# Score matmuls of two heads in alternating row tiles, and vector work moved to ScalarE and GpSimd

## What is computed

```python
h = relu(layernorm(x)); x = x + L0(h)   # deg*(h Wi + b) + A (h Wj)
h = relu(layernorm(x)); x = x + L1(h)   # one-head graph attention
h = relu(layernorm(x)); x = x + L2(h)   # 8-head dot-product attention, masked by adj
h = relu(layernorm(x)); x = x + L3(h)   # 4 attention heads + 1 output head, FFN, layernorm
```

## Time and profile before

| | us |
|---|---|
| median of 3 runs | 1984.97 (1984.79 to 1987.22) |
| the profiled execution | 1986.96 |
| its span, first to last instruction | 1985.3 |
| PE busy | 1872.7 (94% of the span) |
| DVE busy | 1727.5 (87%) |
| ACT busy | 1450.5 (73%) |
| POOL busy | 607.5 (31%) |

### The profile page before, as it was taken

How to read it: one execution, slowest core, us unless ns; L and a number is a source line. 1 busy time by engine, 2 the same in 40 slices (tenths; PEclk the granted TensorE clock), 3 DMA queues, 4 the chain that set the end, 5 groups by cost and what they waited for, 6 DMA issues and landing times.

```text
span 1985.3 us, 45990 instructions
## 1 busy us (share of the span) xinstructions
PE 1872.7 (94%) x15944; PEld 1772.0 (89%) x15944; DVE 1727.5 (87%) x6095; ACT 1450.5 (73%) x3378; POOL 607.5 (31%) x756
## 2 busy tenths in 40 slices
PE   0789999999999999999999999999999999999965
PEld 0789999999999999999999999999999999998864
DVE  6678999999999999999999999999999989999743
ACT  2347787777777877787787777778877777787653
POOL 4112332323333223333332323333223333322222
PEclk8789999999999999999999999999999999999887
DMA  5000000000000000000000000000000000000000
GB/s 158 9 13 11 23 23 17 18 23 13 22 23 23 18 17 23 23 12 22 23 21 19 18 23 12 22 23 23 17 18 23 23 12 23 18 17 18 12 16 11
DMA packets 31206, 43.85 MB, mean 22 GB/s; under 512 B 3328, under 2 KB 26880, under 8 KB 30976
## 3 DMA queue, kind: packets, MB, share of 16 engines
q1 hardware_dynamic: 30976, 40.91, 6.4%
HBM read 32.38 MB, written 8.52 MB: 21 GB/s over the span
## 4 chain that ended last, share of the span: by engine, by line
PE 78%; DVE 8%; ACT 5%; issue 5%; POOL 1%; DMA 0%; DVEq 0%; ACTq 0%; POOLq 0%; SPq 0%
PE ps L900 54%; PE ps L929 13%; PE ps L1094 8%; PE ps L1113 3%; DVE lg L1367 2%; ACT pT L861 2%; ACT ea L808 1%; DVE tb L1296 1%; DVE cx L1387 1%; ACT pb L853 1%; ACT ea L799 0%; PE ps L1002 0%; DVE fu L1333 0%; DVE hT L1220 0%; DVE pT L1375 0%
## 5 line engine op out<-in xcount | busy, mean ns | idle before, releaser
L853 ACT ACTIVATE pb<-lg,hmin 128x256 f32<-128x256 f32 x512 | 232.1, 503 | 67.4 <-DVE hmin L1367 67.0
L1094 PE MATMUL ps<-kp,qp 32*128 32x256 f32 x1536 | 251.7, 296 | 3.3 <-DVE hmin L1367 1.7
L708 POOL TENSOR_SCALAR ea<-ea,rs 128x256 f32<-128x256 f32 x256 | 144.2, 575 | 356.7 <-DVE rs L1317 356.6
L735 POOL TENSOR_TENSOR fu<-fu,b_b 128x256 f32<-128x256 f32 x64 | 45.9, 738 | 674.1 <-PE ps L929 674.1
L861 ACT ACTIVATE pT<-ps 128x512 f16<-128x512 f32 x256 | 151.1, 590 | 133.3 <-PE ps L1113 67.4
L1367 DVE CUSTOM_DVE_ANT_0 lg<-ps,maskp 128x256 f32<-128x256 f32 x512 | 195.3, 419 | 55.6 <-PE ps L1094 55.6
L1094 PEld LDWEIGHTS ps<-kp,qp 32*128 32x128 f32 x1536 | 199.3, 186 | 39.4 <-issue 12.3
L900 PE MATMUL ps<-wout,hid 128*128 128x256 f32 x1536 | 219.7, 289 | 3.3 <-ACT hid L867 2.6
L900 PE MATMUL ps<-pT,whs 128*128 128x256 f32 x1536 | 212.6, 288 | 4.8 <-DVE pT L1326 3.0
L900 PE MATMUL ps<-wh,hT 128*128 128x256 f32 x1536 | 205.0, 286 | 0.4 <-DVE cols L1267 0.3
L692 POOL TENSOR_TENSOR rstd<-ve,pow_half 128x2 f32<-128x2 f32 x160 | 118.4, 741 | 280.4 <-DVE ve L1198 280.3
(11 more groups left out here) (180 smaller groups left out, 4683.3 us busy)
## 6 DMA issues: line engine op xcount, KB each, us to landing
tbc<-t_dram SPq DMA_DIRECT2D x32, 512.0 KB, 3.6
xin<-x_in SPq DMA_DIRECT2D x32, 256.0 KB, 2.8
out<-xs SPq DMA_DIRECT2D x32, 256.0 KB, 2.2
t_dram<-tb SPq DMA_DIRECT2D x128, 1.0 KB
xs<-a_heads SPq DMA_DIRECT2D x4, 128.0 KB, 6.3
pT<-a_heads SPq DMA_DIRECT2D x4, 128.0 KB, 5.0
lg<-W_out SPq DMA_DIRECT2D x2, 256.0 KB, 5.5
tb<-adj SPq DMA_DIRECT2D x1, 256.0 KB, 2.8
```

Source lines behind the costliest of these rows:

```text
L708: last = pool.tensor_scalar(ea(g)[:, c, :], ea(g)[:, c, :], rs[g][:, c:c + 1], 1.0, ALU.mult, ALU.mult)
L853: last = act.activation(pb[h % 2][:, c, :], lg[h % 2][:, c, :], ACT.Exp, bias=hmin[h % 2][:, c:c + 1], scale=-1.0)
L1094: last = pe.matmul(bank(BA)[:, c, :], qp[r, a, oc, blk(c)], kp[r, b, oc, :], start=(n == 0), stop=(n == 2))
```

## The change

The scores of two heads become one step of 12 matmuls. Heads `2p` and `2p+1` alternate matmul by matmul; they lie in neighbouring 32-row tiles of the array, and the odd head writes bank `BB` instead of `BA`. Each head's transposed probabilities go to its own bank (`head_bank`). The pair's scores wait for `pT16_lo` of the pair before; `p_T` waits no longer for the other head. ScalarE writes the normalised rows of the four layers' norms from `rstd` and a new `nmr` (minus mean times `rstd`), which POOL computes with two instructions of one column behind `inv_std`. POOL also takes `normal`, and the low parts of layer 3's last head and of the FFN. `stats` gets a wait for the rows of the batch before at its head. The planner gets costs for all this and new `LEAD` values.

```diff
-            a("inv_std", n, PO, 0.78, ("var", n))
+            a("inv_std", n, PO, 1.1 if n < 4 else 0.78, ("var", n))
...
-            a("rows", 2, VE, 0.65, ("inv_std", 2), ago("rows_T", 3))
+            a("rows", 2, SC, 0.8, ("inv_std", 2), ago("rows_T", 3))
...
-                a("scores", h, TE, 0.7, ("q_lo", 0), ("k_lo", 0), ("smin", h - 1))
-                a("smin", h, VE, 0.69, ("scores", h), ("s_exp", h - 2))
+                if h % 2 == 0:
+                    a("scores", h // 2, TE, 0.8, ("q_lo", 0), ("k_lo", 0), ("pT16_lo", h - 1))
+                a("smin", h, VE, 0.69, ("scores", h // 2), ("s_exp", h - 2))
                 a("s_exp", h, SC, 0.8, ("smin", h), ("p_T", h - 2))
-                a("p_T", h, TE, 0.44, ("s_exp", h), ("pT16_lo", h - 1))
+                a("p_T", h, TE, 0.44, ("s_exp", h))
...
-                    a("normal", h // 2, VE, 0.27, ("gather", h // 2))
+                    a("normal", h // 2, PO, 0.5, ("gather", h // 2))
...
-                a("hid_lo", g, *((VE, 0.7) if g == HG else (PO, 1.25)), ("hid_hi", g))
+                a("hid_lo", g, PO, 1.25, ("hid_hi", g))
...
-            a("f1_lo", 0, VE, 0.7, ("f1_hi", 0))
+            a("f1_lo", 0, PO, 1.25, ("f1_hi", 0))
...
-        GRAIN, LEAD = 0.02, (42.0, 28.0, -2.0, 23.0)
+        GRAIN, LEAD = 0.02, (58.0, 49.0, 48.0, 52.0)
...
+        def head_bank(h):
+            return BB if h % 2 else BA
...
-                    pool.tensor_tensor(rstd[n][:], ve[n][:], pow_half[:], ALU.pow).then_inc(rstd_ready[n], 1)
+                    ins = pool.tensor_tensor(rstd[n][:], ve[n][:], pow_half[:], ALU.pow)
+                    if n < 4:
+                        ins.then_inc(rstd_made[n], 1)
+                        pool.wait_ge(rstd_made[n], u + 1)
+                        for c in range(C):
+                            ins = pool.tensor_scalar(nmr[n][:, c:c + 1], mv[n][:, c, 0:1], rstd[n][:, c:c + 1], -1.0,
+                                                     ALU.mult, ALU.mult)
+                    ins.then_inc(rstd_ready[n], 1)
...
+                def low_of_ffn(_, u):
+                    pool.wait_ge(f1_hi, u + 1)
+                    pool.tensor_tensor(f1p[:, 1], rb5[:], f(f1p[:, 0]), ALU.subtract).then_inc(f1_lo, 1)
+
+                def normalise(p, u):
+                    pool.wait_ge(o_used, of(u, p, HQ // 2))
...
+                        last = pool.tensor_tensor(two_heads(p)[:, hh], two_heads(p)[:, hh],
+                                                 r.broadcast_to([P, C, DH]), ALU.mult)
...
+                def norm_rows(n, u):
+                    t = row_of(n)
+                    act.wait_ge(rstd_ready[n], u + 1)
...
+                    for c in range(C):
+                        last = act.activation(rows_src(t)[:, c, :], norm_src(n, u)[:, c, :], ACT.Identity,
+                                              bias=nmr[n][:, c:c + 1], scale=rstd[n][:, c:c + 1])
+                    last.then_inc(rows_ready[t], 1)
...
-                def scores(h, u):
-                    if h == 0:
+                def scores(p, u):
+                    if p == 0:
                         pe.wait_ge(q_lo, u + 1)
                         pe.wait_ge(k_lo, u + 1)
                     else:
-                        pe.wait_ge(min_ready, of(u, h - 1, HQ))
-                    r, oc = slice(DH * (h % 4), DH * (h % 4) + DH), h // 4
+                        pe.wait_ge(pT16_lo, of(u, 2 * p - 1, HQ))
                     for c in range(C):
                         for n, (a, b) in enumerate(PARTS):
-                            last = pe.matmul(bank(BA)[:, c, :], qp[r, a, oc, blk(c)], kp[r, b, oc, :],
-                                             start=(n == 0), stop=(n == 2))
+                            for h in (2 * p, 2 * p + 1):
+                                r, oc = slice(DH * (h % 4), DH * (h % 4) + DH), h // 4
+                                last = pe.matmul(bank(head_bank(h))[:, c, :], qp[r, a, oc, blk(c)], kp[r, b, oc, :],
+                                                 start=(n == 0), stop=(n == 2))
                     last.then_inc(s_done, 1)
...
                     pe.wait_ge(p_done, of(u, h, HQ))
-                    if h:
-                        pe.wait_ge(pT16_lo, of(u, h - 1, HQ))
-                    transpose_to(BB, pb[h % 2]).then_inc(p_turned, 1)
+                    transpose_to(head_bank(h), pb[h % 2]).then_inc(p_turned, 1)
...
                 def stats_of(n, u):
+                    if n < 4 and u:
+                        dve.wait_ge(rows_ready[row_of(n)], u)
```

90 lines of the change are left out of this document (35 added, 55 removed).

## The result

The changed kernel takes 1937.49 us (median; 1935.54 to 1940.87) against 1985.03: ratio 0.9756, 95% interval 0.9739 to 0.9773. It is faster, by 2.4% and not by the forecast 5.3%. The profiled execution has a span of 1936.5 us.

What follows compares the result with a forecast made beforehand. PE was taken as the bound in mid-run. From a span of 1985.3 us: -46.2 (fewer score groups), -90.6 (overlap), +40 (taken back by others), -10 (end) gave 1878.5, forecast as 1880 us; range 1844 to 1955.

Steps and rivals of the forecast that it cites:

- The view and the bound: Mid-run: PE waits for nobody, 57.8 of 58.0 us a batch; DVE 53.1, ACT 45.3, POOL 18.9.
- Parts 1 and 2: Layer scores on PE: half as many groups, -46.2 us; alternating tiles run two heads side by side, -90.6 us.
- The rivals on the tiles: Score matmuls: loads in series (1934 us, 0.13), no overlap (1946, 0.09), tile changes costing like mode changes (2223, 0.07).
- Part 3: Work leaving DVE: 190.5 us, 6.0 a batch, from 53.1 to 47.1; gains nothing by itself but makes room.
- Part 4: Work arriving elsewhere: ACT 45.3 to 48.9 us a batch, POOL 18.9 to between 23 and 33, staying free.
- Part 5: Mid-run: PE at 53.5 us a batch, ACT 91%, DVE 88%, layer 3's chain 93%; 1.3 us x 31 lost, +40.
- The filling of the pipeline I leave as it is: Start of the run, while the pipeline fills: no separate term in the sum for a change there.
- The bound of 3 us a batch: Upper bound on what other engines and layer 3's chain take back in mid-run, almost the whole overlap; lower bound 0.
- The second rival: Mid-run: overlap works, but layer 3's chain or ACT holds the period at 56.5 us a batch; 1931 us, chance 0.11.
- the sign of its own forecast: Mid-run: PE busy at 97 to 98% and a batch every 54.8 us.
- The signs of being wrong: Mid-run: PE waiting for `pT16_lo` before the scores, or for ACT's normalised rows, would show the prediction wrong.
- Part 6: End of the run: PE's 14.6 us idle between 1880 and 1920 partly filled, 0 to 15 us possible, -10 taken.

Runs made afterwards that it cites:

- the run that removes them: Changed kernel in its own order; from the second batch GpSimd's `hid_lo`, `f1_lo` and beta addition each become two one-column powers: 1897.20 us, ratio 0.9538.
- all three pairs of kernels: Kernel before, pair of scores only, and all of the change, each with old and new `LEAD`: 1985.0 and 2098.07, 2064.06 and 1973.56, 2110.88 and 1937.49 us.

## Why the prediction was wrong

**The view and the bound.** Right that PE held the period before. Right, too, that after the change others would be close behind. The time, 1937.5, lay in the stated range, near its high end.

**Parts 1 and 2, fewer and overlapping scores.** Right. Six score matmuls took 0.97 us and twelve take 0.98. With the holds gone PE is busy 0.984 x 54.7 = 53.8 us a batch, where the prediction had 53.5. The score groups are 128, and what the passage costs is unchanged (below). The rivals on the tiles are refuted: loads in series would give a distance of 0.11 and a price per tile change 0.3; the couples start together.

**Part 3, DVE.** Mis-sized. It took the six groups' own busy time, 190.5 us, for what VectorE would be spared. Neighbouring DVE instructions overlap in the trace (before, their durations sum to 2155.6 us and the busy time is 1727.5), so what a group covers is in part covered by its neighbours: without the 576 instructions of these groups the busy time of before would be 1580.3, only 147.2 us less. The rest of VectorE's work then took 66.1 us more than before, about what the holds added (78.0 - 11.0). So VectorE fell by 147.2 - 66.1 = 81.1 us (2.5 a batch) and not by 190.5 (6.0). "DVE near 1540" was 1646.4.

**Part 4, ACT and GpSimd.** ACT 1546.9 (forecast about 1565). GpSimd's own time, 25.4 us of 56 a batch, lay in the bounds, and "stays free" was true of GpSimd itself. What the part left out is what GpSimd's instructions do to VectorE's. No row of before was asked for that, though its trace has the thing itself: a `tb<-xs,mv,rstd` of 1.37 us, where the median is 0.41, ended 0.15 us after the GpSimd `TENSOR_TENSOR` in which it began. All such time was 11.0 us there, with GpSimd at 31%.

**Part 5, what the others take back.** This is the step that failed, by its size. It took back 1.3 us a batch for queueing; in mid-run 3.1 were taken back (3.12 + 1.3 - 1.29). Of the 1.8 too many, 1.4 went with the holds (56.09 - 54.68): GpSimd's wide instructions held VectorE's, a wait that the prediction put at nothing without a reason. With the holds away the gain is 57.38 - 54.68 = 2.70 of the 3.12 + 1.3 = 4.42 that PE was to save, so 1.7 are taken back: near my 1.3. In all, of the 57 us that were missing the holds are 40 (1937.5 - 1897.2, by the run that removes them, with the open part named there). What still separates that run's span (1899.3) from the forecast's 1878.5 is the stretch up to the 5th batch, 25.7 us longer than forecast (294.99 us), and mid-run with the last four batches, 13.9, against an end that is 19.0 better. "The filling of the pipeline I leave as it is" was the second miss: the new order lengthens it in all three pairs of kernels (by 26, 16 and 14 us). The bound of 3 us a batch was about right, and the range held the time.

**The second rival** (the overlap works, something else holds the period: 1931) is nearest to what happened in its time and its period, 56.5 us for 56.09. That its sum came so close is in part luck: up to the 32nd batch it was 30 us too low and at the end 22 too high. Its sign, PE at 95% or less, didn't show: PE was at 97%, which the prediction had named as the sign of its own forecast. Its mechanism was named too vaguely: not the length of layer 3's chain or ACT's share, but VectorE held beside GpSimd. It got 0.11, which was too little for what a 93% chain through four engines deserved. The signs of being wrong, waits of PE for `pT16_lo` or for ACT's normalised rows in mid-run, didn't show in size: between 500 and 1500 us scores waited 2.7 us in all for `pT16_lo`, and PE not once for normalised rows.

**Part 6, the end.** -32.4 where -10 was said: the right direction, and luck in the size. The new `LEAD` values alone shorten the end by 32.5 us in the kernel before; without these 22 us the time would have been 1960.

**A page that was not weighed.** The Trainium skill ("SBUF — State Buffer", section "Who interferes with whom") says that VectorE and GpSimd share one pair of ports to SBUF as an exclusive lock: a VectorE instruction with two SBUF inputs, or a `tensor_scalar` between SBUF tiles in its faster mode, waits until a GpSimd instruction that started first is done, and one with at most one SBUF input outside those modes doesn't. This case agrees for GpSimd's wide `TENSOR_TENSOR`s. Of 27 masked minima that begin within one, 26 end 0.28 us after its end (the 27th begins 0.06 us before that end). Of 25 of the one-input `tensor_scalar` kind, 24 end 0.15 us after it. Of 147 instructions `lg<-ps,maskp` in the same position (PSUM and one SBUF input) and 34 one-input `BATCH_NORM_STATS2` none is longer. It doesn't agree for GpSimd's powers, which read SBUF too: in the kernel without holds 49 starts of masked minima fall within one, and the longest takes 0.46 us. The rule spoke against moving work from VectorE to GpSimd unseen, and the prediction should have counted which VectorE instructions stand beside which GpSimd ones.

## What to carry over

Work handed from VectorE to GpSimd can come back: 147.2 us of busy time left VectorE here, and its other work took 66.1 more, by the moves and the order together. Count the VectorE instructions with two SBUF inputs, and the `tensor_scalar`s between SBUF tiles, beside GpSimd's wide ones, and keep GpSimd's instructions short or apart from them. When a bounding engine gets lighter and the time follows only in part, sum each group's durations above its median before blaming the longest chain. A high busy share of that engine doesn't clear the others: PE was at 97% with 40 us to be had from VectorE's holds. And in a kernel whose order is laid out by costs, test a part inside the new order as well as the old: the same 44 us of TensorE were worth 12 with the holds and 32 without, and the pair of scores cost 79 us or gained 11 by the order alone.
